# A fused GroupNorm and masked BatchNorm: ScalarE and GpSimd by sets of four images, VectorE in a loop, two stores moved

## What is computed

```
x: (16, 64, 256, 256) float32
g = group_norm(x), 32 groups of 2 channels, mean and variance per image and group
m = g.sum(over channels) != 0                   # per image and place
mean, var over batch and places where m (and padding), per channel
out = where(m, g / sqrt(var + 1e-3), g), place (0,0) also where an image is padded
return x + out
```

## Time and profile before

| | |
|---|---|
| median of 3 runs | 1272.38 us (1269.52 to 1273.73) |
| profiled execution | 1269.24 us, span 1267.5 us |
| TensorE, VectorE, ScalarE, GpSimd busy | 743.8, 767.0, 816.6, 495.3 us |
| moved by DMA | 537.27 MB, mean 424 GB/s |
| mean granted clock of TensorE | 0.779 of full |

### The profile page before, as it was taken

How to read it: one execution, slowest core, us unless ns; L and a number is a source line. 1 busy time by engine, 2 the same in 40 slices (tenths; PEclk the granted TensorE clock), 3 DMA queues, 4 the chain that set the end, 5 groups by cost and what they waited for, 6 DMA issues and landing times.

```text
span 1267.5 us, 10827 instructions
## 1 busy us (share of the span) xinstructions
PE 743.8 (59%) x2882; PEld 299.9 (24%) x2882; DVE 767.0 (61%) x1894; ACT 816.6 (64%) x950; POOL 495.3 (39%) x504
## 2 busy tenths in 40 slices
PE   0677654576545775557754567544675446765475
PEld 0222221222212222212221222212222222222222
DVE  7766656565565656655566555665566655666573
ACT  0887555785557865568655686556865568755685
POOL 0055333453334533344433444334443334433350
PEclk9988777887778876778766887767877778867787
DMA  9999999999999999999999999999999999999998
GB/s 397 413 431 430 430 430 430 432 429 430 431 431 430 429 431 430 430 431 430 431 431 430 431 430 431 432 429 431 427 423 429 425 426 426 425 428 422 383 374 365
DMA packets 39066, 537.27 MB, mean 424 GB/s; under 512 B 4337, under 2 KB 4337, under 8 KB 6897
## 3 DMA queue, kind: packets, MB, share of 16 engines
q1 hardware_dynamic: 22032, 289.42, 54.0%
q10 hardware_dynamic: 16992, 247.47, 45.7%
HBM read 268.44 MB, written 268.44 MB: 424 GB/s over the span
## 4 chain that ended last, share of the span: by engine, by line
DMA 60%; ACT 17%; PE 10%; DVE 6%; issue 5%; SPq 0%; ACTq 0%; DVEq 0%
DMA out_dram<-slots 36%; DMA slots<-in_x_dram 24%; ACT slots L387 12%; PE flush L472 6%; ACT fresh L383 5%; DVE stats L531 2%; PE stay L468 1%; PE small_ps L428 1%; PE stay L469 1%; PE small_ps L441 1%; DVE spread L510 1%; PE small_ps L442 1%; ACT sums L383 0%; DVE dev L577 0%; DVE spread L551 0%
## 5 line engine op out<-in xcount | busy, mean ns | idle before, releaser
L531 DVE BATCH_NORM_STATS2 stats<-slots 128x6 f32<-128x512 f32 x1024 | 632.6, 680 | 436.3 <-DMA slots<-in_x_dram 434.6
L387 ACT ACTIVATE slots<-slots,out_bias,out_scale 128x1024 f32<-128x1024 f32 x512 | 623.4, 1248 | 2.4 <-DVE out_bias L588 1.2
L365 POOL TENSOR_TENSOR sums<-fresh,sums 128x512 f32<-128x512 f32 x360 | 459.4, 1276 | 375.9 <-ACT fresh L383 375.9
L472 PE MATMUL flush<-slots,weights 128*64 128x512 f32 x1488 | 428.8, 698 | 39.8 <-ACT fresh L383 37.7
L383 ACT ACTIVATE fresh<-flush,group_bias 128x512 f32<-128x512 f32 x360 | 247.5, 688 | 51.8 <-PE flush L472 51.8
L472 PEld LDWEIGHTS flush<-slots,weights 128*64 128x64 f32 x1488 | 124.3, 156 | 288.4 <-issue 150.6
L344 POOL TENSOR_TENSOR weights<-pair_sum,group_rstd 128x64 f32<-128x64 f32 x128 | 33.7, 295 | 359.7 <-DVE group_bias L568 359.7
L400 ACT ACTIVATE by_image<-by_image,eps 128x4 f32<-128x4 f32 x32 | 9.5, 298 | 247.3 <-DVE by_image L555 246.6
L468 PE MATMUL stay<-slots,weights 128*64 128x512 f32 x512 | 140.5, 611 | 0.0
L469 PE MATMUL stay<-minus_mean,weights 128*64 128x512 f32 x512 | 138.0, 593 | 0.0
L428 PE MATMUL small_ps<-stats,group_avg 128*128 128x64 f32 x64 | 21.3, 432 | 190.2 <-DVEq L544 190.2
(11 more groups left out here) (56 smaller groups left out, 224.0 us busy)
## 6 DMA issues: line engine op xcount, KB each, us to landing
slots<-in_x_dram SPq DMA_DIRECT2D x127, 2048.0 KB, 19.4
out_dram<-slots ACTq DMA_DIRECT2D x118, 2048.0 KB, 28.0
out_dram<-slots SPq DMA_DIRECT2D x6, 2048.0 KB, 17.2
out_dram<-slots SPq DMA_DIRECT2D x16, 512.0 KB, 9.0
slots<-in_x_dram SPq DMA_DIRECT2D x4, 512.0 KB, 7.5
```

Source lines behind the costliest of these rows:

```text
L365: pool.tensor_tensor(into, fresh[:, n % FRESH_BUFS, :], into, ALU.add).then_inc(added, 1)
L387: nc.scalar.activation(out_in_ring(u, i), image_in_ring(u, i), ACT.Identity, bias=out_bias[:, buf(u), t:t + 1], scale=out_scale[:, buf(u), ...
L472: nc.tensor.matmul(into, weight, source, start=True, stop=True).then_inc(image_summed, 1)
L531: last = V.bn_stats(stats[:, buf(u), k * BLOCK_STATS:(k + 1) * BLOCK_STATS], source)
```

## The change

- ScalarE works by sets: `take(u, t)` drains the three flush banks (now one PSUM tensor, 1536 columns) in one instruction once all three images are summed; `put_out` writes a whole tile (4096 columns) in one. Per unit 4 + 4 instructions for 12 + 16. Unit 31's outputs stay one per image.
- GpSimd adds by sets (1536 columns), makes the weights of a unit in one instruction (two in unit 31), and copies the mean and rstd, which now stand in one of three buffers (`moments`), to a table of all units.
- TensorE's first image of a set waits for the drain of the set before; the order of its images is the same.
- VectorE's units 1 to 30 are a loop of six turns of five units. Its waits inside are for values worked out from the turn. The last block of a unit itself starts TensorE's first small matmul (`small_in`), where a separate wait and increment did.
- The stores of tiles 118 and 119 are ScalarE's, as all before them; SyncE issues those of 120 to 123 after the last loads (`HELD`).

```diff
+        HELD = TILES - 2 * UNIT_TILES
...
-            for j in range(TILES - RING, TILES - UNIT_TILES):
-                sp.wait_ge(out_ready, (j + 1) * TILE_CHUNKS)
+            for j in range(HELD, TILES - UNIT_TILES):
+                sp.wait_ge(out_ready, j + 1)
                 sp.dma_start(in_dram(out_rows, j), tile_in_ring(j)).then_inc(stored[j % RING], 16)
...
-            def take(u, i):
-                t = set_of(i)
+            def take(u, t):
 
                 if u == 0:
-                    into = sums[:, flushed.index(i), :]
+                    into = sums_of(t)
                 else:
...
+                    into = fresh[:, :, :]
+                    if u > 1 or t:
+                        act.wait_ge(added, (u - 1) * SETS + t)
+                wait_for_sum(act, u, t * SIDE + FLUSH_BANKS - 1)
+                nc.scalar.activation(into, flush[:, :, :], ACT.Identity, bias=group_bias[:, buf(u), t:t + 1]).then_inc(taken, 1)
...
                 if u < LAST:
-                    store(u, UNIT_TILES - 1)
+                    for t in range(SETS):
+                        take(u, t)
+                        if t:
+                            store(u, t - 1)
+                        tile = tile_in_ring(u * UNIT_TILES + t)
+                        wait_for_sum(act, u, t * SIDE + SIDE - 1)
+                        put_out(u, t, tile, tile).then_inc(out_ready, 1)
+                    store(u, SETS - 1)
...
-                        if m >= FLUSH_BANKS:
...
+                        bank = bank_of(i)
+                        if u < LAST:
+                            if i % SIDE == 0 and (u or t):
+                                pe.wait_ge(taken, ago * (TURN * SETS) + u * SETS + t)
...
+            def wait_for_step(k):
+                dve.wait_ge(dve_step, turns[0] * (TURN * UNIT_STEPS) + k)
...
+            unit(0, 0)
+            with dve.Fori(0, (UNITS - 2) // TURN) as turn:
+                for u in range(1, 1 + TURN):
+                    unit(u, turn)
+            unit(LAST, 0)
```

More of the change, by code:

```diff
@@ L21 @@
 RING = 10
-FRESH_BUFS = 3
 FLUSH_BANKS = 3
@@ L61, in norm_conv_kernel @@
     ADDS = len(flushed)
+    assert SIDE == TILE_CHUNKS and ADDS == SETS * FLUSH_BANKS and all(set_of(i) * SIDE + FLUSH_BANKS > i for i in flushed)
     SMALLS = 4
@@ L82, in norm_conv_kernel @@
                         for t in (x, out))
[L84 removed]
+    assert TURN * UNIT_TILES % RING == 0 and (UNITS - 2) % TURN == 0
     def buf(u):
[L87 to L93 removed]
+        return (0, 1, 2, 0, 1)[(u - 1) % TURN] if u else BUFS - 1
     ctx = ExitStack()
@@ L494, in _ @@
             V = nc.vector
-            steps = [0]
+            steps, turns = [0], [0]
             def note(ins):
@@ L532, in block_stats, with statistics @@
                 if k == UNIT_BLOCKS - 1:
-                    last.then_inc(summed, 1)
-            def statistics(u, meanwhile):
-                at = slice(u * SETS, (u + 1) * SETS)
-                mean, rstd, bias = group_mean[:, at], group_rstd[:, at], group_bias[:, buf(u), :]
+                    last.then_inc(small_in, 1)
+            def statistics(u, turn, meanwhile):
+                mean, rstd, bias = moments[:, buf(u), 0, :], moments[:, buf(u), 1, :], group_bias[:, buf(u), :]
                 means, squares = triples(u)[:, :, :, 1], triples(u)[:, :, :, 2]
-                dve.wait_ge(summed, u + 1)
-                dve.sem_inc(small_in, 1)
+                steps[0], turns[0] = u * UNIT_STEPS, turn
+                smalls = turn * (TURN * SMALLS) + u * SMALLS
                 meanwhile(1)
-                dve.wait_ge(small_out, u * SMALLS + 1)
+                dve.wait_ge(small_out, smalls + 1)
                 link(V.tensor_reduce(mean, mean_ps.rearrange("p (i f) -> p i f", f=FOLDS), AX_X, ALU.add))
@@ L590, in _, with unit @@
             AHEAD = 6
-            for u in range(UNITS):
+            def unit(u, turn):
                 for k in range(AHEAD if u else 0, UNIT_BLOCKS):
-                    block_stats(u, k)
+                    block_stats(u, k, turn)
                 ahead = [0]
                 def meanwhile(n):
-                    if u + 1 < UNITS:
+                    if u < LAST:
                         for k in range(ahead[0], ahead[0] + n):
-                            block_stats(u + 1, k)
+                            block_stats(u + 1, k, turn)
                     ahead[0] += n
-                statistics(u, meanwhile)
-                assert ahead[0] == AHEAD
+                statistics(u, turn, meanwhile)
+                assert ahead[0] == AHEAD and steps[0] == (u + 1) * UNIT_STEPS
+            unit(0, 0)
[3 more added lines that the diff above has]
+            unit(LAST, 0)
             def count(i):
```

139 lines of the change are left out of this document (57 added, 82 removed).

## The result

The changed kernel takes 1290.05 us at the median (1287.3 to 1296.35, 4 runs), the kernel before 1272.07 us beside it: a ratio of 1.0159, 95% interval 1.0137 to 1.018. It is slower by 18 us between the medians and by 20 us by the ratio, where 11.6 us were forecast. The time lies inside the range given (1269 to 1292), 6 us above the forecast of 1284. The profiled execution took 1289.87 us with a span of 1288.1.

A forecast was written before the change was run, and what follows sets the result against it. The prediction took late DMA engines, one slowed by VectorE's instruction packets, as the bound. Profiled 1269.24 + 0 + 0 + 12.5 = 1281.7 us, 1284.9 with the 3.1 us to the median, rounded down to 1284; range 1269 to 1292.

The forecast's parts named there:

- what bounds the kernel: Whole run: two late DMA engines pace the rest, one delayed by VectorE's instruction packets, 15 x 0.95 = 14 us.
- the number of packets: VectorE's loop: body fetched again each turn, 13.2 packets more; bounds 4.2 packets (+4 us) and 18 (+17 us); chance 0.63.
- the stall at the jump is hidden: VectorE's jumps back: a stall of a few us each, under the 5 us VectorE waits at each tile.
- the price of a packet: DMA engine carrying VectorE's packets: each delays it 0.95 us, so 13.2 x 0.95 = +12.5 us.
- rounded down for packets that may follow each other cheaply: Last step of the sum: 1284.9 us lowered to 1284 us.
- a wide instruction saves nothing: ScalarE's drains and outputs: only the start is saved, a unit stays at 25.1 us.
- the latency of the first drain: ScalarE, start of a unit: first drain waits for three images instead of one, +3.4 us, cost in the middle 0.
- the forecast's 3.6 us later: Tail: first final output near 1239.4 us for 1235.76, last store issue near 1260.3 for 1256.6.
- The held stores: Tail: stores of tiles 118 and 119 leave earlier and fill idle engines; gain 0, from 0 to 5.6 us.
- A (body kept): Rival on VectorE's loop: body fetched once and kept, second late engine sets the pace, 1270 to 1274 us; chance 0.25.
- B (faster): Rival on the tail: late engines don't end the run, 5.6 us idle in 1194 to 1210 come back, 1266.8; chance 0.10.
- C (each unit delayed): Rival on ScalarE: sets of four delay each unit, 1302 us; chance 0.02.

The follow-up runs named there:

- e3: Kernel before with four more already met waits ahead of each VectorE block statistic (2048 instructions, no jump): 1303.06 us, ratio 1.0253.
- e15: Kernel before with a 6 KB row transfer that nothing reads behind every load from tile 10 on, 117 in all: 1318.84 us, ratio 1.0362.
- e1: Changed kernel with VectorE's units 1 to 30 written out in a straight line instead of the loop: 1267.28 us, ratio 0.9974 to before.
- e7: Written-out version of the changed kernel with six small VectorE loops added, ten turns of a ten-instruction body each: 1269.5 us, ratio 1.0008 to before.
- e12: Changed kernel with VectorE's loop written out, run again in more rounds: 1268.78 us, ratio 0.9986 to before.
- e5: Kernel before with two more already met waits ahead of each VectorE block statistic (1024 instructions): 1279.27 us, ratio 1.009.
- e14: Kernel before with four more already met waits at three of every four VectorE block statistics (1536 instructions): 1290.51 us, ratio 1.0155.
- e11: Kernel before with only the stores of tiles 118 and 119 moved to ScalarE's queue: 1269.08 us, ratio 0.9994.

## Why the prediction was right in its mechanism and wrong in its size

**Right: what bounds the kernel.** A late DMA engine slows the rest; e3 shows it with instruction packets, e15 with ordinary transfers. **Right: the number of packets.** The forecast had 13.2 more for the loop, the body fetched again at each jump and a block read in vain. Taking the loop out removes 14 (40 to 26). Queue 14 has 40 packets although ScalarE's and GpSimd's halved (26 in e1 for 37 before), just short of the "over 40" that the forecast named as its sign. Around the first jump back, at 216 to 232 us, after has four of them, e1 one:

```profile
q14 instruction: 4, 0.03, 0.5%
...
q14 instruction: 1, 0.01, 0.1%
```

The Trainium skill, "Runtime: NRT & Kernel Launch", "Instruction fetch mechanics", speaks of a DMA fetch at a taken branch out of the window, and the five stalls of 5.6 us in after, with e7's none, agree with it. The 512 instructions that the prediction cites from it are more than the 391 of the body; the body was fetched again all the same. The same section calls the crossing of a block boundary "mostly hidden". It is, for VectorE, which shows no such stall in e1; for the DMA engine that carries the block it isn't, and here that was the dearer side. **Right: the stall at the jump is hidden** (28.0 us of stalls, the waits for loads stay at 434.6 us).

**Wrong: the price of a packet.** This is the term that was mis-sized: 13.2 x 0.95 = 12.5 us stood in the sum, and 14 packets cost 22 to 24 us (after against e12 and e1, by the ratios), 1.6 us each. The failing step is that 0.95, read from the steps between load issues before 350 us, was multiplied by all packets as if the price were one. As the delay of the one engine it is right (0.84 to 0.95 us by the linked packets); as the price in time of the kernel it isn't one number: by e5, e14 and e3 the first few cost next to nothing more, the later ones near 2.9 us. The range's upper bound of 17 us for 18 packets was too low for the same reason; that the median fell into the range is luck: 3 us for scatter stood on top, and the sets gained 2 to 3. And "rounded down for packets that may follow each other cheaply" went the wrong way. The sign was to be had in before: its rate already sags from 430 to 426 GB/s at the end, the first part of the curve.

**Wrong: "a wide instruction saves nothing".** ScalarE's timeline in unit 29 of after:

```profile
1189.44 3.81 ACT L374 ACTIVATE slots<-slots,out_bias,out_scale 128x4096 f32<-128x4096 f32 x1
1193.15 1.52 ACT L371 ACTIVATE fresh<-flush,group_bias 128x1536 f32<-128x1536 f32 x1
...
1194.57 3.79 ACT L374 ACTIVATE slots<-slots,out_bias,out_scale 128x4096 f32<-128x4096 f32 x1
```

From output to drain it is 3.71 us for 4096 columns, against 4 x 1.14 = 4.56 for four of 1024; from drain to output 1.42 against 3 x 0.57 = 1.71. Columns and a start together: 4a + s = 3.71 and a + s = 1.14 give s = 0.28 us for each instruction. The argument was that half the columns take half the time (0.57 for 1.14). But the two aren't points of one line: for the drains 3a + s = 1.42 and a + s = 0.57 give s = 0.15. The columns cost the same in both, 0.83 to 0.84 ns, and the drain's start is half as long as the output's, which looked like no start at all. The output reads SBUF and has a scale and a bias for each partition, the drain reads PSUM and has a bias alone; no run tells which of the two makes the difference. A unit takes 4 x (3.71 + 1.42) = 20.5 us for 25.1. The gain lies off the path: e1 is 2 to 3 us faster than before, with 137 us less of ScalarE.

**Right: the latency of the first drain.** Two rows of ScalarE's timeline in unit 30 of after, the second root and the first drain, then the first drain in before:

```profile
1222.53 0.26 ACT L388 ACTIVATE col<-small_ps,eps 128x1 f32<-128x1 f32 x1 [4.44 <-PE small_ps L431]
...
1227.84 1.54 ACT L371 ACTIVATE fresh<-flush,group_bias 128x1536 f32<-128x1536 f32 x1 [5.05 <-PE flush L462]
...
1205.32 0.69 ACT L383 ACTIVATE fresh<-flush,group_bias 128x512 f32<-128x512 f32 x1 [1.73 <-PE flush L472]
```

ScalarE waits 5.05 us for the first three images of unit 30, 3.3 us more than for one image, as forecast (3.4). It costs nothing that e1 shows, as forecast.

**The tail.** Load 126 and the outputs at the end, from timelines of after, and then the DMA share in two stretches:

```profile
1217.46 0.54 SPq L262 DMA_DIRECT2D slots<-in_x_dram  x1
```

```profile
1228.15 2.74 SPq L265 DMA_DIRECT2D slots<-in_x_dram  x4
1233.32 15.94 SPq L270 DMA_DIRECT2D out_dram<-slots  x4
1257.49 19.17 SPq L273 DMA_DIRECT2D out_dram<-slots  x16
```

```profile
1217.50:1228.00 10.50, 7.11 (x22) 3.15 (x23) 8.93 (x31) 0.72 (x3) 0.76 (x2) 0.53 1.01 430
1254.00:1259.00 5.00, 5.00 (x18) 1.94 (x18) 2.46 (x9) 3.03 (x4) 0.00 (x0) 0.59 0.38 162
```

Measured from the issue of load 126, which carries the loop's delay, the last sixteen stores begin after 1257.49 - 1217.46 = 40.0 us, against 1237.03 - 1196.0 = 41.0 before; the forecast's 3.6 us later aren't there; ScalarE's unit, 4.6 us shorter than it took, more than makes up for them. Before's gap lay between the issues of the loads 126 and 127 (share 0.65 in 1194 to 1210). Between the same two issues, 1217.5 to 1228 in after, the share is 1.01, so that gap is gone; another has opened at 1254 to 1259 (0.38), before the final stores. The held stores as such are worth nothing that can be measured (e11), as forecast.

**The rivals.** A (body kept) fell by e1 and by the packets. B (faster) holds for the part without the loop, at half its size: 2 to 3 us for 5.6. C (each unit delayed) fell: VectorE's and ScalarE's slack stayed.

**Open.** What makes the second engine late; why loads move slower where few stores go beside them, and whether the late engine causes that mix; why the load packet behind an instruction packet is slow; and how the price would go on beyond 16 packets.

## What to carry to other kernels

Where all DMA engines are busy, ask how evenly they are loaded: a few small transfers that fall on one of sixteen (instruction packets of one engine, single-row transfers) cost next to nothing until it lags by the queued work, and then more than their own duration (here 2.9 us a packet of 0.309 us, which delays its engine by some 0.9 us). A price read early in this kernel, in the flat stretch, was a lower bound; look at the rate in slices and find where it starts to sag. VectorE's loop with a body of 391 instructions was fetched again on every turn (14 packets more in all than written out, near the forecast of five a turn for 2.5), while one of ten wasn't. So in a kernel that is bound by its DMAs, try a long loop body against straight code.

## What the runs showed of the hardware

- Padding in VectorE's code (2048 instructions that do nothing) costs 33 us in a kernel in which VectorE waits 464.7 us for loads (e3); as many in ScalarE's cost 3 to 6, in GpSimd's -0.5 to 3. Their packets take different DMA engines (linked packets), and a packet of VectorE delays its engine by 0.84 to 0.95 us, one of the others by 0.5 to 0.7.
- 0.13% more bytes, all on one DMA engine, cost 3.6% of the time (e15).
- Where loads outweigh stores two to one a load takes 47 us of one DMA engine a MB, else 37 (the dip at 757.5 us of after), and the rate is 350 GB/s for 430.
- Each instruction of ScalarE has a start beside its columns, worked out from two lengths of each: 0.28 us for an output (SBUF, scale and bias), 0.15 us for a drain (PSUM, bias alone).
